# Six products of a tile of ones ahead of the first transposes

## The reference

```python
x = L0_attn_x
x = x + _L0_attn_ref(_layernorm(x), Wq, bq, Wk, bk, Wv, bv, Wo, bo)
x = x + _L0_ffn_ref(_layernorm(x), rW1, rb1, rW2, rb2, We1, be1, We2, be2)

# in _L0_attn_ref: Q = x @ Wq.T + bq, and K and V likewise
scores = einsum("bhqd,bhkd->bhqk", Q, K) / sqrt(hd)
A_stable = 0.6 * softmax(scores) + 0.4 * L
out = einsum("bhqk,bhkd->bhqd", A_stable, V) @ Wo.T + bo
```

## Time and profile before

| | |
|---|---|
| median of 3 runs | 1991.34 us (1990.6 to 1992.51) |
| profiled execution, first to last instruction | 2006.8 us |
| TensorE busy | 1951.3 us, 97% |
| VectorE busy | 1626.5 us, 81% |
| ScalarE busy | 1374.2 us, 68% |
| GpSimd busy | 346.9 us, 17% |
| mean granted clock of TensorE | 0.995 |

### The profile page before, as it was taken

One profiled execution on the slowest core, in us unless ns is written; L12 is line 12 of the kernel. 1 busy time (PEld: TensorE's weight loads), 2 busy tenths in 40 slices (PEclk: granted clock), 3 DMA queues, 4 the chain that ended last, 5 costly groups with the idle time before them and its releaser, 6 DMA issues. The chain is left out here.

```text
span 2006.8 us, 47862 instructions
## 1 busy us (share of the span) xinstructions
PE 1951.3 (97%) x16384; PEld 1036.7 (52%) x16384; DVE 1626.5 (81%) x2075; ACT 1374.2 (68%) x2471; POOL 346.9 (17%) x379
## 2 busy tenths in 40 slices
PE   7999999999999999999999999999998799999997
PEld 3543333333333333333333333333687689999997
DVE  6799999999999999999999999994255565555564
ACT  3358888888888888888888888889544422233332
POOL 1361010001000100001000100010024532232233
PEclk9999999999999999999999999999999899999999
DMA  7954355335643454336534554341123677788884
GB/s 266 245 111 92 78 102 115 74 74 97 108 90 74 90 99 106 74 80 102 113 74 74 100 105 90 74 93 54 42 74 131 242 235 227 245 269 297 263 272 113
DMA packets 105849, 264.09 MB, mean 132 GB/s; under 512 B 20896, under 2 KB 52768, under 8 KB 99104
## 3 DMA queue, kind: packets, MB, share of 16 engines
q1 hardware_dynamic: 92624, 245.29, 48.6%
q0 software_dynamic: 13152, 17.83, 4.6%
HBM read 206.95 MB, written 73.94 MB: 140 GB/s over the span
## 5 line engine op out<-in xcount | busy, mean ns | idle before, releaser
L626 DVE TENSOR_REDUCE part_max<-psum 128x1 f32<-128x1024 f32 x1024 | 1240.8, 1222 | 50.6 <-PE psum L750 37.7
L681 ACT ACTIVATE probs<-psum 128x512 f32<-128x512 f32 x2048 | 1111.1, 596 | 145.4 <-PE psum L763 78.2
L763 PE MATMUL psum<-score_q,score_k 50*128 50x512 f32 x2048 | 745.9, 446 | 0.1
L750 PE MATMUL psum<-max_k,max_q 48*128 48x512 f32 x2048 | 737.9, 449 | 0.5 <-DVE part_max L626 0.4
L775 PE MATMUL psum<-probs,v_ones 128*32 128x256 f32 x8192 | 654.1, 391 | 9.4 <-ACT heads_sb L696 9.0
L763 PEld LDWEIGHTS psum<-score_q,score_k 50*128 50x128 f32 x2048 | 306.9, 184 | 404.7 <-ACT probs L681 390.7
L775 PEld LDWEIGHTS psum<-probs,v_ones 128*32 128x32 f32 x8192 | 162.1, 107 | 380.8 <-issue 198.1
L750 PEld LDWEIGHTS psum<-max_k,max_q 48*128 48x128 f32 x2048 | 294.2, 185 | 12.8 <-issue 7.0
L1184 ACT ACTIVATE x_sb<-psum,x_sb 128x512 f32<-128x512 f32 (+1 forms) x160 | 101.6, 636 | 257.8 <-PE psum L1564 243.1
L1583 PE MATMUL psum<-w,h_hi 128*128 128x256 f32 x1120 | 202.1, 279 | 2.7 <-DVE h_lo L1385 2.5
L1583 PEld LDWEIGHTS psum<-w,h_hi 128*128 128x128 f32 x1120 | 178.7, 189 | 13.8 <-DVE h_lo L1385 3.2
(11 more groups left out here) (185 smaller groups left out, 1352.3 us busy)
## 6 DMA issues: line engine op xcount, KB each, us to landing
w<-w_split SPq DMA_DIRECT2D x40, 2048.0 KB, 7.9
max_q<-qk_pieces SPq DMA_DIRECT2D x192, 128.0 KB, 7.2
score_k<-qk_pieces SPq DMA_DIRECT2D x192, 128.0 KB, 4.7
xs<-in_pads SPq DMA_DIRECT2D x33, 528.0 KB, 8.3
qk_pieces<-pieces SPq DMA_DIRECT2D x32, 512.0 KB, 4.6
w_split<-w_pair SPq DMA_DIRECT2D x32, 512.0 KB, 8.8
max_k<-qk_pieces SPq DMA_DIRECT2D x192, 64.0 KB, 8.2
score_q<-qk_pieces SPq DMA_DIRECT2D x192, 64.0 KB, 2.2
```

The source lines that it names most:

```text
L626: nc.vector.tensor_reduce(part_max[:, t, p:p + 1], ps_m[p].rearrange("q b f -> q (b f)"), axis=AXIS.X, op=ALU.max).then_inc(m_read, 1)
L681: nc.scalar.activation(probs[kb % 2][:, chunk * BLOCK:(chunk + 1) * BLOCK], bank_of(at), ACT.Exp, scale=float(HD) ** -0.5).then_inc(exp_do ...
L750: last = nc.tensor.matmul(ps_m[p][:, h, :], max_q[u][rows, t * P:(t + 1) * P], max_k[u][rows, p * BLOCK:(p + 1) * BLOCK], start=True, stop ...
L763: nc.tensor.matmul(bank_of(at), score_k[u][rows, kb * P:(kb + 1) * P], score_q[u][rows, part * BLOCK:(part + 1) * BLOCK], start=True, stop ...
```

## The change

GpSimd fills a tile `blank` of 128x512 float32 with ones, ahead of its other work, and signals `blank_set`. TensorE waits for it and computes six products of the tile with its own first 128 columns into PSUM bank 3, ahead of the wait for the identity. Nothing reads that bank before `attend` starts it anew.

```diff
+WARMUP = 6
@@ project
     half = sb("half", [P, BT])
+    blank = sb("blank", [P, BLOCK])
@@
     ps_qk = [psum[:, 4 + j, :] for j in range(2 * KD)]
+    ps_blank = psum[:, 3, :]
@@
+    blank_set = sem("blank_set")
@@ GpSimd
+        nc.gpsimd.memset(blank[:], 1.0).then_inc(blank_set, 1)
         nc.gpsimd.memset(half[:], -0.5).then_inc(pool_set, 1)
@@ TensorE
+        pe.wait_ge(blank_set, 1)
+        for _ in range(WARMUP):
+            nc.tensor.matmul(ps_blank, blank[:, 0:P], blank[:], start=True, stop=True)
         pe.wait_ge(ident_in, 16)
         transposes(0, 0)
```

## The result

| | before | changed |
|---|---|---|
| median | 1991.19 us | 2136.07 us |
| lowest to highest of 6 runs | 1990.6 to 1992.51 | 2128.51 to 2147.73 |
| ratio, 95% interval | | 1.0731 (1.0706 to 1.0756) |
| profiled execution, span | 2006.8 us | 2131.4 us |

The change makes the kernel 7.3% slower, 145 us, where 3.2 us less were forecast. Here is the timeline of the first 20 us of the changed kernel (start, length, engine, line, tiles, count, and the idle time before with its releaser).

The account below looks back on a forecast made before the run. TensorE, busy 97% of the span, was taken as the bound. Savings 0.90 + 2.87 = 3.77 us with a late clock rise, 2.6 with an early one; middle 3.2, so 1991.34 - 3.2 = 1988.1 us, range 1985.6 to 1991.0.

Parts of the forecast that it names:

- (a): Start, GpSimd: filling the tile of ones ends at about 1.3 us; cost 0, without cover 0.5 us.
- (b): Start, TensorE: the wait for the tile holds back nothing that could run before 9.61 us; cost 0.
- (c): Start: six products, counted as twelve, end at 8.2 to 9.4 us, hidden by VectorE's work; uncovered up to 8.1 us.
- (d): First block's transposes run at the full clock, 1.04 us in place of 1.94; saves 0.90 us.
- (e): First q products take 3.44 us in place of 6.31, ending at 15.3 in place of 19.07; saves 2.87 us.
- (f): Projection after the first q products: later inputs, biases and stores do not become the bound.
- (g): Rest of projection and attention: the gain lasts to the end, since loads, stores and waits follow TensorE; no loss.
- prediction's own sign of being wrong: TensorE begins later than 1.5 us, or the shift differs between the ends of projection and attention.
- the slower one: Start: the six products never bring the higher clock, so transposes begin 2.0 us late; 1993.4 us, chance 0.05.
- something that no row shows (code placement, ...): No place named: an unseen effect, large in either direction, such as code placement or changed transfer order; chance 0.04.
- Rival 1: Start: clock falls again between the six products and the q products; gain 0.9 to 2.1 us, chance 0.2.
- Rival 4: From 1430 us on: one low-clock restart more or fewer, about 1.7 us each, 1989.8 or 1986.4; no separate chance.

Follow-up runs that it names:

- places 52 and 60: Kernel before, attention loop's first TensorE instruction set at number 52 or 60 of a 256-instruction block: 1991.22 us; 2075.12 us profiled, 2114.19 the other run.
- place 16: Attention loop's first TensorE instruction set at number 16 of a 256-instruction block: changed kernel with six products 1989.16 us, kernel before 1990.6 us.

## Why the prediction was wrong, point by point

- **What bounds the kernel**: right that TensorE is the chain. It follows that whatever stops TensorE in a loop costs in full, which was not turned against the change.
- **(a), (b), (c)**: right in time. Tile set at 1.24 us, products over at 8.98, forecast 8.2 to 9.4. Wrong by omission in (c): "six are twelve" counted only what the trace counts as products. With the weight loads they are 24 instructions of code, and the place that they take in TensorE's program was priced at nothing.
- **(d), (e)**: right. 1.06 us of transposes, q products from 11.75, the next transposes at 15.26 (forecast 15.3). In the changed kernel the clock held between. The seven profiled executions without early products have their second transposes at 17.88 to 19.27, the three with six products and fast q products at 15.26 to 15.38: 2.5 to 4.0 us earlier, where the forecast had 2.6 to 3.8.
- **(f)**: right; the projection ended 3.81 us earlier than in the profiled execution before, at 72.89 (forecast 72.9).
- **(g)**, "Behind it TensorE is full for 1353 us. I take no loss": this is the step that failed. It asked only whether a transfer, a store or another engine would eat the gain. The attention loop's code had moved by 24 instructions, and its 1736 instructions no longer fit in seven blocks of 256. Each of 14 jumps back then waited about 4 us and left TensorE at the lower clock behind it: 10.4 us a jump (145.2 / 14) in place of 0. The prediction's own sign of being wrong, a shift that is not the same at the end of the attention, says so: TensorE was 3.81 us early at the start of that stage and 141.3 us late at its end (1567.83 in place of 1426.49). Without the stalls the step holds as far as it was argued: with the jump announced the attention takes 1350.0 us, with 1349.8 before.
- **The rivals**: the slower one (ones that never bring the clock) was a mechanism of 2 us in the first 12 us; the real one was not among them. It stood only in "something that no row shows (code placement, ...)", at 0.04 with no price and no place. One row could have led to it: the page's instruction packets, 44 of 16.4 KB, say that no code was fetched twice in a loop that is nearly as large as its seven blocks, so that a shift can only leave this as it is or harm. The Trainium skill, "Runtime: NRT & Kernel Launch", Instruction fetch mechanics, says that TensorE holds 2048 instructions, refilled in blocks of 256, and that a taken branch to code that isn't held stalls for a fetch. The runs agree with the blocks of 256 (the border between places 52 and 60, and no stall 240 instructions on) and with the stall, 3.95 us. The same section of the Trainium skill calls the window about the branch two pages; there the runs differ, since a loop of nearly seven blocks jumped back with no wait and no packet more, and the measurement decides.
- **Rival 1** (0.2, gain 0.9 to 2.1): not in the changed kernel's profile, but seen with the head at place 16, where the gain was 1.4 to 2.2, and with three products, where nothing measurable was left.
- **Rival 4** (the last stage lands differently) is real too. In all profiled executions but that of the kernel before, the stretch behind the attention took 562.9 to 565.5 us, a scatter of 2.6 us against a gain of 3. With the jump announced it took 565.5: TensorE was 2.9 us ahead of the kernel before at place 16 when the attention ended (1422.89 against 1425.75), and only 0.4 us at the end (1988.4 against 1988.8).
- **The size of the gain**, 3.2 us, was too large even with the stalls gone. Six products gave 2.2 us at place 16, 1.2 with the jump announced and 1.1 as a hardware loop (two of its 13 runs stalled), and only the first is clear of no change. The 3.4 us of the run with a seventh product belong to another change. The start was worth what the sum says when the q products were fast; what rival 1 and rival 4 each took of it on the mean is open.

What stays open is the inside of the fetch. A loop that reaches four to sixteen instructions into its eighth block is fetched anew in full (8 or 9 packets a jump), although eight blocks are no more than the 2048 instructions of that page of the Trainium skill, and with the jump announced nothing is fetched again. This would fit a ninth block that is fetched ahead of the jump and pushes out the first; no run shows which block goes. Where exactly the loader puts the first instruction of the kernel before isn't known either, only the estimate above for its loop's head.

## What to carry to other kernels

Instructions are not free because they run in idle time: on TensorE every instruction ahead of a long loop moves its body against the fetch blocks. Here a body that just fitted into seven blocks lost about 10 us at each jump back, most of it by the clock, when it reached into an eighth; bodies of other lengths and loops of other engines were not run. Count the loop's instructions, compare the instruction packets of the page with the size of the program before and after an edit, and look for waits with no releaser at the loop's head. Where the language allows it, fix the loop's place or announce the jump first, and only then judge a small edit.

## What the runs showed of the hardware that was not expected

- The cost of a jump back that stalled was 3.8 to 4.3 us of standstill on TensorE in the changed kernel (up to 5.0 in the other runs) and, with the lower clock behind it, 10.4 us in all; the clock's part, 93.2 us, was larger than the waits', 55.7 us.
- The border isn't sharp: 4 instructions into the eighth block 9 of 14 jumps stalled in the profiled execution, 16 into it all did.
- Waits that are already met still cost TensorE time: 216 instructions of two waits each held the transposes back by 15.4 us, 72 to 110 ns an instruction.
- Announcing the jump at the loop's head removed not only the waits but all 126 repeated packets.
- Three products that ended at 6.79 us, 2.74 us ahead of the transposes, still left these at the full clock (1.06 us), and the q products behind them at the lower one.
